# Causal mask of the first attention: from a TensorE product to an addend of VectorE

## The reference, cut to what matters

```python
scores = jnp.einsum('bhqd,bhkd->bhqk', qf, kf) * scale
causal = jnp.tril(jnp.ones((s, s), dtype=bool))
scores = jnp.where(causal, scores, jnp.finfo(scores.dtype).min)
probs = jax.nn.softmax(scores, axis=-1)
o = jnp.einsum('bhqk,bhkd->bhqd', probs, v)
```

## Time and profile before

| what | value |
|---|---|
| median of 3 runs | 2464.71 us (2463.24 to 2464.78) |
| the profiled execution's own time | 2451.58 us |
| its span | 2449.8 us |
| TensorE busy over the span | 2207.0 us (90%) |
| VectorE busy | 1495.8 us (61%) |
| ScalarE busy | 1276.5 us (52%) |
| GpSimd busy | 596.0 us (24%) |
| stage of `mla_heads` | first product at 200.35 us, last output multiplied at 831.95 us |

### The profile page before, as it was taken

One profiled execution on the slowest core, in us unless ns is written; L12 is line 12 of the kernel. 1 busy time (PEld: TensorE's weight loads), 2 busy tenths in 40 slices (PEclk: granted clock), 3 DMA queues, 4 the chain that ended last, 5 costly groups with the idle time before them and its releaser, 6 DMA issues. The chain is left out here.

```text
span 2449.8 us, 34913 instructions
## 1 busy us (share of the span) xinstructions
PE 2207.0 (90%) x12768; PEld 1290.9 (53%) x12768; DVE 1495.8 (61%) x2176; ACT 1276.5 (52%) x2133; POOL 596.0 (24%) x496
## 2 busy tenths in 40 slices
PE   5797999999999799999999959799999999999877
PEld 4565777777777575444444334234444444444443
DVE  2575777777777434579999754359999821113253
ACT  4464667776777421248888842038888842100321
POOL 1464666666666301130000013000000000001210
PEclk9898999999999899989999979899999999999888
DMA  2782111111111321140010010601121030000010
GB/s 77 235 251 65 53 57 55 56 56 52 59 53 48 111 78 45 55 107 21 21 40 21 2 69 22 167 26 27 27 45 36 2 139 20 0 0 0 0 31 35
DMA packets 82920, 138.72 MB, mean 57 GB/s; under 512 B 31201, under 2 KB 41185, under 8 KB 82802
## 3 DMA queue, kind: packets, MB, share of 16 engines
q1 hardware_dynamic: 82802, 137.11, 19.1%
HBM read 95.65 MB, written 41.03 MB: 56 GB/s over the span
## 5 line engine op out<-in xcount | busy, mean ns | idle before, releaser
L2379 POOL TENSOR_TENSOR l0a_p_low<-yT,l0a_p_high 128x1024 fp32r<-128x1024 f32 (+7 forms) x256 | 389.1, 1538 | 237.7 <-ACT l0a_p_high L2403 236.0
L198 POOL TENSOR_TENSOR applied<-prepared,neghalf 128x2 f32<-128x2 f32 x64 | 50.6, 791 | 1384.3 <-DVE prepared L160 1384.3
L1656 DVE TENSOR_REDUCE l2a_mx<-ps 128x2 f32<-128x1024 f32 x256 | 310.4, 1224 | 56.2 <-PE ps L1470 55.5
L1656 DVE TENSOR_REDUCE l1a_mx<-ps 128x2 f32<-128x1024 f32 x256 | 310.0, 1224 | 38.4 <-PE ps L1470 37.6
L1611 ACT ACTIVATE l1a_prob<-ps 128x512 f32<-128x512 f32 x512 | 278.3, 596 | 66.5 <-PE ps L1489 47.8
L1611 ACT ACTIVATE l2a_prob<-ps 128x512 f32<-128x512 f32 x512 | 278.3, 596 | 62.9 <-PE ps L1489 43.0
L2441 DVE TENSOR_REDUCE l0a_mx<-ps 128x1 f32<-128x512 f32 (+3 forms) x384 | 206.3, 551 | 76.2 <-PE ps L2284 55.2
L2456 DVE TENSOR_TENSOR yT<-ps,l0a_mrows 128x1024 f32<-128x1024 f32 (+7 forms) x256 | 192.9, 754 | 88.5 <-PE ps L2308 80.8
L2397 ACT ACTIVATE yT<-yT 128x1024 f32<-128x1024 f32 (+7 forms) x256 | 175.1, 684 | 116.9 <-DVE yT L2456 116.9
L2403 ACT CAST l0a_p_high<-yT 128x1024 fp32r<-128x1024 f32 (+7 forms) x256 | 172.5, 674 | 14.3
L2284 PE MATMUL ps<-l0a_k_high,l0a_q_high 128*128 128x512 f32 (+3 forms) x384 | 143.0, 387 | 35.3 <-DVE l0a_mx L2441 23.7
(11 more groups left out here) (306 smaller groups left out, 3929.7 us busy)
## 6 DMA issues: line engine op xcount, KB each, us to landing
l0a_q<-l0a_q SPq DMA_DIRECT2D x32, 512.0 KB, 3.3
l0q_woh<-in_l0a_wo SPq DMA_DIRECT2D x16, 512.0 KB, 4.9
l0a_q<-f SPq DMA_DIRECT2D x32, 256.0 KB, 4.7
l0a_q<-l0q_q_pe SPq DMA_DIRECT2D x32, 256.0 KB, 3.7
l0a_recip_rows<-l0a_recip_row SPq DMA_DIRECT2D x32, 256.0 KB, 3.4
l0a_o<-l0a_o_pair SPq DMA_DIRECT2D x16, 512.0 KB, 2.8
yT<-l0a_o SPq DMA_DIRECT2D x16, 512.0 KB, 3.3
l2a_k<-l2a_k_parts SPq DMA_DIRECT2D x16, 256.0 KB, 4.4
```

The source lines that it names most:

```text
L1656: nc.vector.tensor_reduce(mx[:, u % 2, :, p, t, c], banks(("pair", m)), AX.X, ALU.max).then_inc(s_red, 1)
L2379: nc.gpsimd.tensor_tensor(p_low[:, j % 4, P * j:T], prob[:, j % 4, P * j:T], p_high[:, j % 4, P * j:T], ALU.subtract).then_inc(s_pl, 1)
```

## The change

The mask leaves the products of the second pass. At the start of the stage one product of `mask` and `unit` puts the turned mask in PSUM, and VectorE copies it to a tile `mask_keys`. Once a head VectorE adds this tile to all eight 128-column tiles of `mrows` and keeps the result as `masked_rows` (128 x 1024, two buffers); it waits for its own instruction. `less_max` is split in two for tiles 0 to 6: the 128 columns of the diagonal tile take `masked_rows`, the rest `mrows`; tile 7, which has the diagonal tile alone, stays one instruction. `less_max(h, 0)` now waits for `mrows` before it waits for the scores. The mask products of the first pass (L2288) stay.

```diff
--- before.py
+++ after.py
@@ -2198,12 +2198,13 @@
     p_high, p_low = sb("p_high", [P, 4, T], F32R), sb("p_low", [P, 4, T], F32R)
     oT = sb("o_pair", [P, T])
     osum = sb("osum", [KV_RANK + 1, T])
+    masked_rows, mask_keys = sb("masked_rows", [P, 2, T]), sb("mask_keys", [P, P])
     rows8, recip8 = sb("rows8", [P, NT]), sb("recip8", [P, NT])
     recip_row = nc.dram_tensor("l0a_recip_row", (T,), F32).ap()
     (s_high, s_mm, s_red, s_neg, s_mt, s_mrow, s_less,
-     s_low, s_st, s_exp, s_pv, s_os, s_r8, s_rd, s_rst, s_rb, s_on) = (chip.sem("l0h_" + n) for n in (
+     s_masked, s_turned_mask, s_kept_mask, s_low, s_st, s_exp, s_pv, s_os, s_r8, s_rd, s_rst, s_rb, s_on) = (chip.sem("l0h_" + n) for n in (
          "q_high",
-         "max_scores", "reduced", "negated", "max_turned", "max_rows", "less_max", "q_low", "scores", "exps", "pv", "o_out", "sums_spread", "recip", "recip_stored",
+         "max_scores", "reduced", "negated", "max_turned", "max_rows", "less_max", "masked_rows", "mask_turned", "mask_kept", "q_low", "scores", "exps", "pv", "o_out", "sums_spread", "recip", "recip_stored",
          "recip_loaded", "o_done"))
     ST = [ps[:, 0:2, :].rearrange("p b n -> p (b n)"), ps[:, 2:4, :].rearrange("p b n -> p (b n)")]
     O = ps[:, 4:6, :].rearrange("p b n -> p (b n)")
@@ -2301,13 +2302,10 @@
                     pe.wait_ge(s_low, h - 1)
                 for lo, hi in spans(j):
                     out = ST[j % 2][:, lo:hi]
-                    diagonal = lo == P * j
                     keys = slice(j * P, (j + 1) * P)
                     nc.tensor.matmul(out, k_high[:, keys], q_high[:, par, lo:hi], start=True, stop=False)
                     nc.tensor.matmul(out, k_high[:, keys], q_low[:, par, lo:hi], start=False, stop=False)
-                    mm = nc.tensor.matmul(out, k_low[:, keys], q_high[:, par, lo:hi], start=False, stop=not diagonal)
-                    if diagonal:
-                        mm = nc.tensor.matmul(ST[j % 2][:, lo:lo + P], mask[:], unit[:], start=False, stop=True)
+                    mm = nc.tensor.matmul(out, k_low[:, keys], q_high[:, par, lo:hi], start=False, stop=True)
                 mm.then_inc(s_st, 1)
 
             def pv(h, j):
@@ -2354,11 +2352,13 @@
                         pv(h, j - 1)
                     chunks(j, 2)
 
+            nc.tensor.matmul(ST[0][:, 0:P], mask[:], unit[:], start=True, stop=True).then_inc(s_turned_mask, 1)
             for n in range(NMAX):
                 max_chunk(0, 0, n, True, True)
             max_turn(0, 0)
             for n in range(AHEAD):
                 max_chunk(1, 1, n, False, True)
+            pe.wait_ge(s_kept_mask, 1)
             scores(0, 0, 0, True)
             scores(0, 0, 1, True)
             head(0, 0, first=True)
@@ -2446,15 +2446,25 @@
 
             def less_max(h, par, j, first=False):
 
+                if j == 0:
+
+                    dve.wait_ge(s_mrow, h + 1)
+                    nc.vector.tensor_tensor(masked_rows[:, par, :].rearrange("p (t q) -> p t q", q=P),
+                                            mrows[:, par, :].rearrange("p (t q) -> p t q", q=P),
+                                            mask_keys[:].unsqueeze(1).broadcast_to([P, NT, P]),
+                                            ALU.add).then_inc(s_masked, 1)
+                    dve.wait_ge(s_masked, h + 1)
                 dve.wait_ge(s_st, h * NT + j + 1)
-                if j == 0:
-                    dve.wait_ge(s_mrow, h + 1)
                 if not (first and j < 4):
 
                     dve.wait_ge(s_ph, h * NT + j - 3)
                     dve.wait_ge(s_pl, h * NT + j - 3)
-                nc.vector.tensor_tensor(prob[:, j % 4, P * j:T], ST[j % 2][:, P * j:T], mrows[:, par, P * j:T],
-                                        ALU.add).then_inc(s_less, 1)
+                own = slice(P * j, P * j + P)
+                mm = nc.vector.tensor_tensor(prob[:, j % 4, own], ST[j % 2][:, own], masked_rows[:, par, own], ALU.add)
+                if j < NT - 1:
+                    mm = nc.vector.tensor_tensor(prob[:, j % 4, P * j + P:T], ST[j % 2][:, P * j + P:T],
+                                                 mrows[:, par, P * j + P:T], ALU.add)
+                mm.then_inc(s_less, 1)
 
             def invert(h):
                 dve.wait_ge(s_r8, h * 16 + 16)
@@ -2494,6 +2504,9 @@
                         for n in range(AHEAD):
                             reduce_chunk(h + 2, par, n)
 
+            dve.wait_ge(s_turned_mask, 1)
+            nc.vector.tensor_copy(mask_keys[:], ST[0][:, 0:P]).then_inc(s_kept_mask, 1)
+            dve.wait_ge(s_kept_mask, 1)
             for n in range(NMAX):
                 reduce_chunk(0, 0, n)
             negate(0)
```

More of the change, by code:

```diff
@@ L2447, in less_max @@
             def less_max(h, par, j, first=False):
-                dve.wait_ge(s_st, h * NT + j + 1)
                 if j == 0:
                     dve.wait_ge(s_mrow, h + 1)
+                    nc.vector.tensor_tensor(masked_rows[:, par, :].rearrange("p (t q) -> p t q", q=P),
[3 more added lines that the diff above has]
+                    dve.wait_ge(s_masked, h + 1)
+                dve.wait_ge(s_st, h * NT + j + 1)
                 if not (first and j < 4):
```

## The result

The changed kernel takes 2479.86 us (median of 20 runs, 2467.92 to 2492.02), the kernel before, run beside it, 2467.78 us (20 runs, 2450.34 to 2479.33): ratio 1.0057, 95% interval 1.0041 to 1.0073. It is slower, by about 14 us by the ratio (12 us by the two medians), where 8 us less were forecast. The profiled execution took 2484.02 us.

What follows compares the result with a forecast made beforehand. TensorE sets the pace, but meets VectorE at each head's negation. Mean gain 0.29 us over 31 transitions, -9.0, plus 1.1 once, gives -7.9 off median 2464.71: 2456.8 us; own range 2452 to 2461, whole range 2450 to 2470.

Steps and rivals of the forecast that it cites:

- The chain: Waits TensorE and VectorE share from less_max(1) to the negation: 0.35 us less in one head, 0.23 in the next.
- What TensorE saves: Second-pass mask products removed: 0.11 us each, eight a head, 0.88 us a head as upper bound of the gain.
- rival 4: Splits cost nothing and the add ends before its scores: 0.55 us a head, 2449 us; chance 0.07.
- The split at 0.07 us: Cutting 128 columns off less_max costs VectorE 0.07 us each, seven a head, 0.46 us.
- Rival 1: Each split of less_max costs its full 0.15 us: 2466 us, no change; chance 0.15.
- plus 0.04 us for the wait on itself: VectorE's wait for its own add, before less_max(0), costs 0.04 us, the distance read from the negation's held start.
- Bounds 1.21 and 1.55; I take 1.21: Duration of VectorE's add making masked_rows, between finish and less_max(0): taken as 1.21 us, like L2435.
- rival 2: The add collides with GpSimd's part of tile 7 and takes 1.55 us: 2462 or 2467 us; chance 0.17.
- Waits of TensorE: Before max_turn growing from 0.05 to some 0.3 us; before chunks 2 and 5 staying about 0.8 and 0.5 to 0.6.
- Once only: Costs outside the repeated heads: 0.8 us more at the stage's end, 0.3 us at its start.
- Rival 3: Slower: add at 1.55 us and splits at 0.15 together, VectorE bounding the whole head: 2477 us; chance 0.13.

Runs made afterwards that it cites:

- product_out_alone: Changed kernel without the add and the split, less_max whole, second-pass mask left out; steps 18.37 and 18.64 us, ratio 0.9953 when timed.
- own_wait_last: Changed kernel with VectorE's wait for its own add put behind the other three waits of less_max(0); steps 18.68 and 19.37 us.
- add_reads_psum: Changed kernel with the add taking the maxima from PSUM instead of mrows, chunk 0 waiting for it; steps 18.83 and 19.23 us.
- second timing: The changed kernel timed again, against the kernel before, beside a timing of the kernel before against itself; ratio 1.0046.
- the crossed version: Changed kernel with the add in two halves from PSUM ahead of finish, VectorE and ScalarE's copy exchanging banks; ratios 0.9995 and 0.9975.
- the control: The kernel before, unchanged, timed against itself to check the comparison; ratio 0.9993.

## Why the prediction was wrong

The direction was wrong, and the result lies above the range. The chain was the right one. The step that failed is the price of the add between `finish` and `less_max(0)`: 1.21 + 0.04 us were put there, and it measured 1.21 + 0.29 us in one head and 1.53 + 0.29 us in the next. A fall of the clock, for which no term stood, came on top.

- **What TensorE saves**: right. Without the product, and nothing added, a step is 0.60 us shorter (product_out_alone), and of the other 0.28 us some 0.2 are seen as longer waits of TensorE for VectorE (0.12 before `max_turn`, 0.10 more at chunk 5). Its rival 4, that all costs of VectorE vanish, put 0.55.
- **The split at 0.07 us**: right. Three on the path cost 0.21 us a step; the hand-over after 0.20 us is in the rows. Rival 1 falls: the second half of `less_max` starts 0.08 us before the 0.28 us of the first are over (523.25 to 523.46: 0.21 us). Of the two sections of the Trainium skill's page "VectorE: DVE Perf Modes" weighed there, the trace agrees with "Two Vector instructions with no wait between them".
- **"plus 0.04 us for the wait on itself"**: failed in the 26 heads of the loop. The 0.04 us were read from the negation, which waits for VectorE's own reduction and has nothing more behind that wait. The wait itself costs as much behind the add, as the written-out heads show (0.04 us). What the forecast left out are the three instructions of the sequencer between it and `less_max(0)`: 0.29 us in all.
- **"Bounds 1.21 and 1.55; I take 1.21"**: failed in every second head, where it is 1.53. Both ends were right, the choice was not: the forecast took the row of L2435, an instruction that runs beside GpSimd without harm to itself, while rival 2 had the order of starts right and was given 0.17. But L2435 did not go unharmed because the two share; it had started first, and GpSimd paid. This row of the kernel before stands beside it (517.71):

```profile
517.96 1.57 POOL L2379 TENSOR_TENSOR l0a_p_low<-yT,l0a_p_high 128x256 fp32r<-128x256 f32 x1 [0.64 <-ACT l0a_p_high L2403]
```

  The same instruction takes 0.74 us in the one head in which no two-input instruction of VectorE runs beside it, and 1.57 us or more in the others. It is an exclusive use, and the one that starts first has it; the trace of the kernel before had shown it. The Trainium skill, "SBUF — State Buffer", section "Who interferes with whom", says that a VectorE instruction with two SBUF inputs contends with GpSimd's SBUF reads, and that the one that comes second blocks for the whole instruction of the first. The trace agrees (2.05 us for a 0.28 us add), and the prediction did not weigh it.
- **The chain, worked again** with 0.29 and 1.53 us: short step -0.35 + 0.25 = -0.10 us, measured -0.14. Long step -0.23 + 0.25 + 0.32 = +0.34, measured +0.31. The chain's arithmetic holds.
- **A fall of the granted clock**: not foreseen. It costs 1.04 us each (20.57 less 19.53), five times 5.2 us. It comes only in long steps, in about a third of those with a wait of 1.54 us at chunk 2 and in two of the eleven with 1.37 us (own_wait_last). None is seen in the short steps, with 1.10 us, nor behind the 0.79 us of the kernel before, nor behind the 1.22 us in the long steps of add_reads_psum. That the wait is what brings it down is inferred from this order.
- **Waits of TensorE**: before `max_turn` 0.18 us instead of the 0.3 forecast. Before chunk 2, where "about 0.8" stood, 1.10 us in a short step and 1.54 in a long one: TensorE comes 0.23 us earlier there, counted from the negation, by the two masks before it; the reduction comes 0.08 us later in the short step and some 0.5 in the long one.
- **Once only**: from the last negation to the end of the last `finish` 1.0 us more (0.8 were forecast), at the start of the stage 0.3 more, as forecast.

Added up over the 31 steps of the profiled execution: 15 short ones bring -2.4 us, the second step -0.4, the 14 long ones +4.2 without and another +5.2 by the clock's falls, that is +9.4 together; the first step +1.1, where the clock fell in this profile and not in the two others (21.96 and 21.92 us against 22.16 before). In all +7.8, and +1.3 with both ends, against 9.1 us measured. Rival 3, which had the sign, is right in the add's place but not in its price: the splits didn't cost 0.15.

**The layers behind the stage** are the same code in both kernels, and this part is open. In the profile they took 1616.6 us before and 1643.8 after, and nearly all of the 27 us lies in the second and third attention. The windows of the second attention in both, first the kernel before:

```profile
991.70:1428.30 436.60, 412.37 (x3368) 178.13 (x3370) 350.22 (x356) 307.55 (x580) 32.31 (x34) 0.98 0.15 38
```

and the changed kernel, with a stretch of its beginning:

```profile
997.20:1449.00 451.80, 426.55 (x3371) 181.26 (x3370) 350.41 (x356) 307.54 (x580) 32.29 (x34) 0.94 0.15 36
...
1077.00:1117.00 40.00, 36.44 (x184) 14.53 (x183) 27.90 (x26) 18.39 (x37) 8.58 (x13) 0.59 0.17 54
```

The products and VectorE's work are the same; the granted clock stays near the lower level for a longer time at the beginning, though TensorE is busy 36.44 of 40 us there. Over all profiles this part varied from 1616.6 to 1649.8 us, and by 20 us between two executions of one kernel, so a pair of profiles says little of it. But it isn't without order: the three profiles of the kernel before have 1616.6 to 1627.0 us, the three of the changed one 1643.1 to 1646.5. By the timings the change costs 14 us (second timing 11.5) against 6 to 9 us in the stage; product_out_alone and the crossed version also lost some 5 us between stage and total, the control nothing. Each of these differences lies within or near its interval. That something of the order of 5 us arises behind the stage is likely, its cause was not found.

## What to carry to other kernels

An instruction added on an engine that has idle time is free only up to the event for which the engine was idle, and in each kind of iteration separately: price it in the worse one. A VectorE instruction with two SBUF inputs costs up to the whole GpSimd instruction that it meets; take one input from PSUM where it is there, and do the work ahead of, not behind, the point where both engines of the chain meet. When an instruction runs unharmed beside another engine, look at what the other one took. Keep further waits out of the place between an instruction and the one that needs its result: ahead of the first they cost nothing here (0.04 us), behind the wait for it they cost 0.25 us.

## What was not expected of the hardware

- VectorE's wait for its own result costs 0.04 us by itself. Each register or wait instruction that the sequencer has to work off between it and the instruction that needs the result costs some 0.08 us, although it is already met (0.29 less 0.04, over three; with one it is 0.13 us).
- GpSimd and a VectorE instruction with two inputs in SBUF exclude each other for whole instructions: 0.28 us became 2.05, 0.47 us became 1.44, 1.21 became 1.53. With one input in PSUM neither was longer in any of 32 heads.
- A wait of 1.54 us in an otherwise full stream of products was followed in about a third of the cases by a stretch at 1.2 GHz that cost 1.04 us, one of 1.37 us in two of eleven, one of 0.79, 1.10 or 1.22 us in none.
- Two executions of one kernel can differ by 20 us with the same instructions (1624.0 and 1644.1 us behind the stage, product_out_alone), at a granted clock of 0.954 and 0.942 over the whole.
